# Four chained layers on one core: K/V of the last pairs ahead of their queries at the change of phase

## The reference

```python
x = x + (einsum('bsi,bio->bso', x, W[id]) + b[id])                  # one of 16 experts per sequence
x = x + (x @ W1.T + (x @ A[a].T) @ B[a].T * s[a])                   # W1 shared, adapter a per sequence
x = x + attention(x)                                                # grouped queries, paged cache
x = x + (w3[subject].T mixes the 64 tokens of a sequence) + bias
```

## Time and profile before

| | |
|---|---|
| median of 3 runs | 934.08 us (932.72 to 934.34) |
| profiled execution | 935.61 us, span 933.8 us |
| PE / DVE / ACT / POOL busy | 890.7 / 648.5 / 442.8 / 529.0 us |
| chain that ended last | PE 77%, DVE 7%, DMA 6% |
| mean granted clock | 0.991 |

### The profile page before, as it was taken

The page is one execution under the profiler, slowest core; times in us unless marked ns, Lnnn a source line. Parts: engine busy times, 40 slices in busy tenths (PEclk is TensorE's granted clock), DMA queues, the critical chain, the costliest instruction groups (busy, mean ns, idle before and its releaser), DMA issues.

```text
span 933.8 us, 23545 instructions
## 1 busy us (share of the span) xinstructions
PE 890.7 (95%) x6501; PEld 654.8 (70%) x6501; DVE 648.5 (69%) x1858; ACT 442.8 (47%) x1190; POOL 529.0 (57%) x499
## 2 busy tenths in 40 slices
PE   5599999999999999999996899999999999999997
PEld 3357667666666676676676677878778778777785
DVE  3545445778787764466755778888778887787874
ACT  1424333333333333333423666666666676666762
POOL 2044655655746557865467666655666656666630
PEclk9889999999999999999999999999999999999999
DMA  9999988787887978887716766676766776666741
GB/s 285 300 285 333 332 303 294 258 286 258 264 291 241 295 252 273 307 269 263 250 64 214 209 205 193 194 211 189 214 194 193 210 222 206 198 199 202 227 133 47
DMA packets 100417, 218.55 MB, mean 234 GB/s; under 512 B 30187, under 2 KB 36168, under 8 KB 92178
## 3 DMA queue, kind: packets, MB, share of 16 engines
q1 hardware_dynamic: 66290, 145.27, 47.4%
q0 software_dynamic: 25088, 57.74, 21.5%
q10 hardware_dynamic: 8992, 15.00, 4.4%
HBM read 210.39 MB, written 33.86 MB: 262 GB/s over the span
## 4 chain that ended last, share of the span: by engine, by line
PE 77%; DVE 7%; DMA 6%; SPq 3%; issue 3%; ACTq 2%; ACT 2%; POOL 1%; DVEq 0%; POOLq 0%
PE banks L697 14%; PE banks L847 9%; PE banks L610 9%; PE banks L799 9%; PE banks L835 7%; PE banks L822 6%; PE banks L678 5%; PE banks L776 4%; DMA pair_b<-in_lb 4%; PE banks L883 3%; PE banks L840 3%; DVE later L1166 2%; PE banks L663 2%; PE banks L777 1%; PE banks L815 1%
## 5 line engine op out<-in xcount | busy, mean ns | idle before, releaser
L569 POOL DMA_INDIRECT ring<-new_rows,idx x128 | 129.3, 1010 | 81.1 <-PE banks L799 45.8
L1050 ACT ACTIVATE big<-big,neg_max 128x320 f32<-128x320 f32 x256 | 141.5, 555 | 4.7 <-DVE neg_max L1417 4.4
L1417 DVE CUSTOM_DVE_ANT_0 big<-banks,mask 128x320 f32<-128x320 f32 x256 | 114.6, 486 | 23.6 <-PE banks L799 22.5
L610 PE MATMUL banks<-ring 128*64 128x512 f32 x512 | 119.5, 609 | 11.5 <-DMA ring<-in_w 11.5
L497 POOL TENSOR_TENSOR rms<-ss,neg_half 128x12 f32<-128x12 f32 x30 | 68.5, 2283 | 70.3 <-DVE ss L1356 70.3
L1040 ACT ACTIVATE kt<-banks 128x384 f32<-128x384 f32 x128 | 61.8, 483 | 92.9 <-PE banks L777 92.8
L495 POOL TENSOR_TENSOR ring<-ring 128x512 f32<-128x512 f32 x30 | 38.7, 1291 | 87.4 <-DVE ring L1237 87.4
L558 POOL DMA_INDIRECT ring<-new_rows,idx x64 | 61.5, 961 | 47.0 <-PE banks L822 42.7
L799 PE MATMUL banks<-kt,q_in 64*128 64x128 f32 (+2 forms) x768 | 86.7, 358 | 1.3 <-ACT kt L1040 1.3
L1454 DVE TENSOR_SCALAR big<-big,recip 128x320 f32<-128x320 f32 x256 | 85.7, 397 | 2.3
L610 PEld LDWEIGHTS banks<-ring 128*64 128x64 f32 x512 | 35.0, 140 | 68.8 <-issue 67.5
(11 more groups left out here) (172 smaller groups left out, 2011.3 us busy)
## 6 DMA issues: line engine op xcount, KB each, us to landing
ring<-in_w SPq DMA_DIRECT2D x62, 1024.0 KB, 8.0
ring<-in_xt SPq DMA_DIRECT2D x32, 256.0 KB, 2.7
x_in<-in_x SPq DMA_DIRECT2D x32, 256.0 KB, 5.8
bias_in<-in_b SPq DMA_DIRECT2D x64, 128.0 KB, 8.0
x_dram<-x SPq DMA_DIRECT2D x32, 256.0 KB, 8.8
q_dram<-q_t ACTq DMA_DIRECT2D x32, 256.0 KB, 6.5
new_rows<-kv_out SPq DMA_DIRECT2D x32, 256.0 KB, 6.4
q_in<-q_dram SPq DMA_DIRECT2D x32, 256.0 KB, 2.8
```

The lines of the kernel that those rows point to most:

```text
L569: pool.indirect_dma_start(out=kv[:, s, c, :], out_offset=None, in_=new_rows, in_offset=bass.IndirectOffsetOnAxis(ap=idx[:, b, 1 + c:2 + c] ...
L610: last = nc.tensor.matmul(ps_l0[T * h:T * h + T, :], xt[:, s, c, T * h:T * h + T], w0[:, 2 * s + h, c * D:(c + 1) * D], start=(c == 0), st ...
L1050: nc.scalar.activation(prob[:, s % 2, PLACE[g] * NK:(PLACE[g] + 1) * NK], sm[:, s % 2, g, :], ACT.Exp, bias=neg_max[:, s % 2, g:g + 1], sc ...
L1417: V.tensor_tensor_reduce(sm[:, s % 2, g, :], ps_s[g], mask[:, s % 2, k0:k0 + NK], 1.0, 3.0e38, ALU.add, ALU.min, accum_out=neg_max[:, s % ...
```

## The change

The end of phase one is written anew. LATE = 29 names the first of the last three pairs. K/V of pairs 29 to 31 are computed and stored first; the query products of these pairs stand behind them, and their rotations and transposes follow; those of pairs 30 and 31 stand partly inside the batches 0 to 2. To make that possible, several things change places: the query products of 30 and 31 go to other banks; the turned x2 of pair 30 gets a buffer of its own (`held_hi`, `held_lo`), for which the second row buffer now shares memory with `same`; the row preparation (make_rows, shift_rows, transposes, indices) goes one step earlier; the own half of the mask is loaded once into `own_mask` and written by ScalarE; the 74 dummies become 14; the splits of Wo go into batches 1 and 2; `bd` is cleared later.

```diff
-ROW_STEP = NP - 5
+ROW_STEP = NP - 6
+LATE = NP - 3
-WARM, WARM_X, WARM_T, WARM_Q, WARM_KEYS = 9, 6, 6, 24, 26
+WARM, WARM_X, WARM_T, WARM_KEYS = 9, 6, 6, 14
-        rows = [sb(f"rows{i}", [P, ROWLEN]) for i in range(2)]
+        rows = [sb("rows0", [P, ROWLEN]), same[:, :, :].rearrange("p m r -> p (m r)")[:, 0:ROWLEN]]
...
 (SyncE)
+            sp.dma_start(own_mask, a["own"]).then_inc(ld_mask, 16)
...
-            for s in range(2):
-                sp.dma_start(mask[:, s, 0:T], a["own"]).then_inc(ld_mask, 16)
-                sp.dma_start(mask[:, s, NK:], a["own"]).then_inc(ld_mask, 16)
...
 (GpSimd; steps of phase one no longer finish pairs 29 and up)
+            last_pow(NP - 3, 1)
             make_table(NP - 1, 1, NP // 2)
-            last_pow(NP - 2, 8, 12, 1)
             pool.wait_ge(idx_ready, 1)
+            pool.wait_ge(l0_done, NP - 1)
+            for b in range(KV_EARLY - 2):
+                gather_old(b)
+            last_pow(NP - 2, 1)
             pool.wait_ge(l0_done, NP)
-            for b in range(KV_EARLY - 1):
+            for b in range(KV_EARLY - 2, KV_EARLY):
                 gather_old(b)
-            last_pow(NP - 1, 8, 12, 3)
-            gather_old(KV_EARLY - 1)
-            last_pow(NP - 2, 0, 8, 2)
-            pool.wait_ge(h_done, NP)
-            pool.wait_ge(kv_done, NP)
-            pool.wait_ge(q_done, NP)
-            nc.gpsimd.memset(bd[:, :, :], 0.0).then_inc(pool_set, 1)
-            last_pow(NP - 1, 0, 8, 4)
+            last_pow(NP - 1, 1)
+            pool.wait_ge(st_kv[0], NP // 2 * 16)
+            last_pow(NP - 3, 0)
...
-            for s in range(2):
-                pool.wait_ge(st_kv[s], NP // 2 * 16)
+            pool.wait_ge(st_kv[1], NP // 2 * 16)
             gather_new(0)
+            pool.wait_ge(q_done, NP)
+            nc.gpsimd.memset(bd[:, :, :], 0.0).then_inc(pool_set, 1)
             for b in range(1, NB):
                 gather_new(b)
+                if b <= 2:
+                    last_pow(NP - 3 + b, 0)
...
 (TensorE, behind step 30)
+            adapt_down(NP - 2, 0)
+            experts(NP - 1, NP // 2 - 1, 1)
+            adapt_up(NP - 2, 0)
+            project_kv(NP - 3)
+            transpose_x1(NP - 1, 1)
+            transpose_x2(NP - 2, 0)
+            transpose_queries(NP - 4, 0)
+            project_q(NP - 3, (0,))
             adapt_down(NP - 1, 1)
-            project_kv(NP - 2)
+            project_hidden(NP - 1)
+
             adapt_up(NP - 1, 1)
-            project_q(NP - 2, (0, 1))
+            project_kv(NP - 2, (0, 1))
             transpose_x2(NP - 1, 1)
-            project_q(NP - 2, (2,))
+            project_kv(NP - 2, (2,))
             project_kv(NP - 1)
+            project_q(NP - 3, (1, 2))
+            project_q(NP - 2)
+            project_q(NP - 1)
             transpose_queries(NP - 3, 1)
-            project_q(NP - 1)
             pe.wait_ge(x1_ready, NP)
-            keep_warm(WARM_Q)
-            transpose_queries(NP - 2, 0)
-            keep_warm(WARM_Q)
-            transpose_queries(NP - 1, 1)
+            keep_warm(WARM_KEYS)
...
 (TensorE, end of a batch's step)
+                if isinstance(b, int) and 1 <= b <= 2:
+                    transpose_queries(LATE + b, (LATE + b) % 2)
+                if isinstance(b, int) and b == 2:
+                    pe.wait_ge(qt_ready, NP)
...
 (ScalarE; the queries of 30 and 31 are copied and stored at the end of its steps 1 and 2)
+            for k0 in (0, NK):
+                last = nc.scalar.activation(mask[:, :, k0:k0 + T], own_mask.unsqueeze(1).to_broadcast([P, 2, T]), ACT.Copy)
+            last.then_inc(mask_set, 1)
...
 (VectorE)
-            SIDE = {2: take_tables, ROW_STEP: make_rows, NP - 1: take_indices}
+            SIDE = {2: take_tables, ROW_STEP: make_rows, NP - 2: take_indices}
...
+            def turn(k, w):
+
+                last_squares(k, w)
+                rotate_parts(k, k % 2, w)
+                last_sum(k, w)
...
+            split_x2(NP - 1)
+            turn(NP - 2, 1)
+            last_product(NP - 2, 1)
+            turn(NP - 1, 1)
+            last_product(NP - 1, 1)
+            turn(NP - 3, 0)
+            last_squares(NP - 2, 0)
+            last_product(NP - 3, 0)
             rotate_parts(NP - 2, 0, 0)
...
             last_sum(NP - 2, 0)
...
 (VectorE, end of a batch's step)
+                if isinstance(b, int) and b <= 1:
+                    last_product(LATE + 1 + b, 0)
+                if isinstance(b, int) and b == 0:
+                    turn(NP - 1, 0)
+                if isinstance(b, int) and 1 <= b <= 2:
+                    for c in range(2):
+                        split_wo(2 * b - 2 + c)
```

More of the change, by code:

```diff
@@ L159, in build @@
             x1t_hi, x1t_lo, x2t_hi, x2t_lo = (sb(n, [P, DC, P], F32R, first) for n in ("x1t_hi", "x1t_lo", "x2t_hi", "x2t_lo"))
+            held_hi, held_lo = (sb(n, [P, DC, P], F32R, first) for n in ("held_hi", "held_lo"))
         q_in = sb("q_in", [P, 4, GP, P])
@@ L255, in is_last, with late, q_bank, kv_bank @@
             return isinstance(pair, int) and pair == NP - 1
+        def late(k, first=LATE):
+            return isinstance(k, int) and k >= first
+        def q_bank(k):
+            return (ps_kv, ps_l1)[k - LATE - 1] if late(k, LATE + 1) else ps_q
+        def kv_bank(k):
+            return ps_t1 if late(k, NP - 1) else ps_kv
+        def turned_bank(k):
+            return (ps_la, ps_l1, ps_l1)[k - LATE] if late(k) else ps_t3
+        def x2t_parts(k):
+            if late(k, NP - 1):
+                return x1t_hi, x1t_lo
+            return (held_hi, held_lo) if late(k, NP - 2) else (x2t_hi, x2t_lo)
         def on(n, lag, count):
@@ L403, in phase_two @@
             def phase_two(b, j, s):
+                if isinstance(b, int) and b == 4:
+                    for t in range(2):
+                        sp.wait_ge(st_q[t], (NP // 2 - t) * 16)
+                if isinstance(b, int) and b == 2:
+                    sp.wait_ge(pool_set, 3)
                 if s % 2 == 0 and on(b, -2, NB):
@@ L476, in make_table @@
                 pool.wait_ge(ld_cs[s], CS_DMAS * 16 * loads)
[L477 to L478 removed]
+                if not late(k, NP - 1):
+                    wait(pool, abq_ready, k - 1)
+                    wait(pool, abk_ready, k - 1)
                 if isinstance(k, int) and k == 0:
                     pool.wait_ge(gains_ready, 1)
[L481 removed]
+                out = last_tab if late(k, NP - 1) else tab[:, s, :, :, :]
+                nc.gpsimd.tensor_tensor(out.rearrange("p w f n -> p w (f n)"),
                                         gains[:, :, :, :].rearrange("p w f n -> p w (f n)"),
@@ L641, in transpose_queries @@
                 wait(pe, qt_ready, k)
+                if late(k, LATE + 1):
+                    pe.wait_ge(abq_ready, NP)
+                    pe.wait_ge(sqq_ready, NP)
+                elif late(k):
+                    pe.wait_ge(xa_ready, NP)
+                out = turned_bank(k)
                 for c in range(DC):
-                    last = nc.tensor.transpose(ps_t3[:, c * P:(c + 1) * P], q_rot[:, s, c * P:(c + 1) * P], ident[:, :])
+                    last = nc.tensor.transpose(out[:, c * P:(c + 1) * P], q_rot[:, s, c * P:(c + 1) * P], ident[:, :])
                 last.then_inc(t3_done, 1)
@@ L687, in project @@
             def project(k, ps_out, n0, parts):
-                x_hi, x_lo = (x1t_hi, x1t_lo) if isinstance(k, int) and k == NP - 1 else (x2t_hi, x2t_lo)
+                x_hi, x_lo = x2t_parts(k)
                 if 0 in parts:
@@ L701, in project_q @@
             def project_q(k, parts=(0, 1, 2)):
-                if 0 in parts:
+                if late(k, NP - 1):
+                    pe.wait_ge(x2_ready, NP)
+                elif late(k, NP - 2):
+                    pe.wait_ge(abk_ready, NP - 1)
+                    pe.wait_ge(sqv_ready, NP - 1)
+                elif 0 in parts:
                     wait(pe, abq_ready, k)
@@ L708, in project_q, with project_kv @@
                         pe.wait_ge(wqkv_lo_ready, 1)
-                last = project(k, ps_q, 0, parts)
+                last = project(k, q_bank(k), 0, parts)
                 if 2 in parts:
                     last.then_inc(q_done, 1)
-            def project_kv(k):
-                wait(pe, abk_ready, k)
-                wait(pe, sqv_ready, k)
+            def project_kv(k, parts=(0, 1, 2)):
+                if late(k, NP - 1):
+                    pe.wait_ge(x1lo_ready, NP)
+                elif 0 in parts:
+                    wait(pe, abk_ready, k)
+                    wait(pe, sqv_ready, k)
                 if isinstance(k, int) and k == 0:
@@ L719, in project_kv @@
                     pe.wait_ge(wqkv_lo_ready, 2)
-                project(k, ps_kv, D, (0, 1, 2)).then_inc(kv_done, 1)
+                last = project(k, kv_bank(k), D, parts)
+                if 2 in parts:
+                    last.then_inc(kv_done, 1)
             def phase_one(k, j, s):
```

199 lines of the change are left out of this document (110 added, 89 removed).

## The result

The changed kernel takes 940.72 us (median of 7 runs, 939.55 to 945.21); the kernel before, measured beside it, 933.91 (median of 7, 931.42 to 936.61). The ratio is 1.0071, 95% interval 1.0049 to 1.0092: slower, by 6.8 us. The forecast was 941.9 in 935.0 to 946.5. The profiled execution took 940.93 us.

The account below looks back on a forecast made before the run. TensorE is full on both sides, so any delay ahead of the full batches delays the end. Terms -7.1 + 5.5 - 1.0 + 2.0 + 6.9 + 1.5 = +7.8 gave 941.9 us, range 935.0 to 946.5.

Parts of the forecast that it names:

- the two places: Places left open near the change: the change of phase (13.9 us gap) and the start of the batches (TensorE works 21.34 of 27.5).
- part 1: End of phase one: pair 31's K/V ready earlier, so the gather starts and the keys come earlier, -7.1 us.
- Part 2: Step 26: row preparation one step earlier makes VectorE wait for table_i and TensorE for x1t_lo, +5.5 us.
- the -1.0 of the next step: Step after the stall: shift_rows finds its adapter rows already there, so TensorE's earlier 0.99 us loss goes, -1.0 us.
- Part 3: Phase one behind the stall: TensorE's granted clock drops after the pause, +2.0 us (1.7 to 2.8).
- Parts 4 and 5: First batches: query work in VectorE's queue delays them, +6.9 us; the pause before the keys costs clock, +1.5 us.
- VectorE's 1.9 and 1.25: Work behind batch 1's mask (a product, two wo_lo quarters), 1.9 us, and behind batch 2's, 1.25, counted as delay.
- the clock would cost one batch 1.5 us: First batch: after a 4.8 us rest before the keys, transposes and scores run up to twice as long, +1.5 us.
- 60 fewer dummies cost nothing: Change of phase: fewer dummies cost and give nothing, as all stand before the same wait for the gather.
- Rival 2: First batches: the clock stays low until the full batches, 3 us more than the sum, 945 us; chance 0.13.
- 6.65 was written: VectorE's work added behind the masks of batches 0 to 2: 3.5, 1.9 and 1.25 us, in all 6.65.

Follow-up runs that it names:

- experiment 1: Changed kernel with the writer-table store and the eleven gathers of table_i one GpSimd step earlier: 935.51 us, ratio 1.0010 to the kernel before.
- experiment 2: Kernel before with only the row preparation one step earlier (ROW_STEP at 26): 938.49 us, ratio 1.0051 to the kernel before.
- experiment 6: Changed kernel with 38 dummies on TensorE before the wait for x1t_lo in step 26: 941.73 us (4 runs), ratio 1.0083 to the kernel before.
- kernel 5: Changed kernel with pair 30's product and pair 31's turn ahead of the first masks, GpSimd's powers for both one batch earlier: 940.24 us, ratio 1.0062.
- experiment 4: Changed kernel with the Wo splits moved from batches 1 and 2 to behind the first mask: 940.86 us, ratio 1.0060 to the kernel before.
- experiment 3: Changed kernel with 36 dummies before the keys instead of 14: 938.94 us, ratio 1.0046 to the kernel before.
- 7: Changed kernel with table gathers a step earlier, 38 dummies before the keys, Wo splits and queries of pairs 30 and 31 ahead: 931.24 us, ratio 0.9981.
- 8: Changed kernel with table gathers a step earlier, 38 dummies before the keys and Wo splits ahead, queries left inside the batches: 933.71 us, ratio 0.9991.
- 9: Changed kernel with table gathers a step earlier, 38 dummies and queries of pairs 30 and 31 ahead, Wo splits left in the batches: 934.23 us, ratio 0.9998.
- kernel 10: Changed kernel with table gathers a step earlier, Wo splits and queries of pairs 30 and 31 ahead, 14 dummies kept: 931.69 us, ratio 0.9972.

## Why the prediction was right, and where it was not

The direction, the two places and the waits in them were as written. That the number came within 1.2 us is in part luck. By the trace the change is worth 5.3 us with the start's -1.8 in it, 7.1 without, where 7.8 was written. The terms behind it were off in both directions: part 1 gave 1.6 us more than forecast and the stall with its clock cost 1.0 less, while the first batches cost 0.6 more and the full batches 1.3, which the sum did not have at all.

**Part 1, the order at the end (-7.1 forecast, -8.7 measured).** The end of pair 31's K/V came 4.9 us earlier, 4.75 forecast (its 2.85 us for twelve matmuls is from start to start; to the end of the last they are 3.01). The gather started 7.1 us earlier once the shift of 3.7 us at that point is taken off (496.21 against 499.60), as forecast, though by two errors that cancel: the store was issued 0.6 us later than written (492.6) and landed in 3.3 us instead of 4.0. The rest is the gather's flight to the keys, 5.83 us instead of 7.41. GpSimd, as forecast, was through with the query power in time, and waited for the store's landing:

```profile
493.53 1.64 POOL L568 TENSOR_TENSOR rms<-ss,neg_half 128x8 f32<-128x8 f32 x1 [1.67 <-DVE ss L1336]
496.21 1.03 POOL L593 DMA_INDIRECT ring<-new_rows,idx  x1 [1.05 <-DMA new_rows<-kv_out]
```

One wait was not foreseen. ScalarE's copy of pair 31's values (timeline of ScalarE after) waits for pair 29's store to leave the same buffer, which had been issued at 483.9:

```profile
490.43 0.39 ACT L1021 ACTIVATE kv_out<-banks 128x256 f32<-128x256 f32 x1 [1.26 <-DMA new_rows<-kv_out]
```

That store took 6.5 us to land, where pair 29's took 2.0 before. From its issue to the place of pair 31's copy it was 5.3 us, 6.2 before, so most of this wait is the slow landing and the smaller part the denser order. I had walked only the store of pair 31.

**Part 2, the stall (+5.5 forecast).** The idle was 4.69 us; place, chain and releaser were as written. With the clock behind it and the -1.0 of the next step, 6.5 in the forecast, it is worth 5.2 by experiment 1, 4.5 by experiment 2. The gathers landed at 406.3 instead of 408.9, but VectorE and TensorE were 1.8 us earlier in this execution, so the stall came out only 0.8 short. The -1.0 was met in size, not in its place: step 27 took 0.4 us more than before, and then the waits for x1t_lo of 0.99, 0.31 and 0.27 us in steps 28 to 30 shrank to a single one of 0.27.

**Part 3, its clock (+2.0).** 1.5 by the groups in experiment 6, or 1.8 by the trace of after (6.5 less 4.69 of idle). It is not the same in every execution: in kernel 5 the same stall, 4.74 us of idle, was followed by 7.92 us from the third part to adapt_up, against 6.70 after and 5.05 before, so there it cost 2.9. (Experiment 1 gets both back and loses the -1.0 again: 6.5 less 1.0 is 5.5, and 5.2 was measured.)

**Parts 4 and 5, the first batches (+8.4 forecast, +9.0 measured).** The sum was right, the account of it in part. Batch 1 came 3.5 us late, and 3.53 of query work stood on VectorE in front of its mask, as forecast. For batches 2 and 3 I had added VectorE's 1.9 and 1.25. They did come 2.2 and 1.6 late, but experiment 4 shows that at batch 2 taking the 1.28 away changes nothing: beside VectorE's queue ran a second chain as long, TensorE at half clock. In kernel 1, where the clock was back at 1.00 by 518, VectorE's queue alone sets the mask of batch 2, without idle and 7.89 us behind batch 1's, 1.8 more than before:

```profile
518.21 1.28 DVE L1488 TENSOR_TENSOR wo_lo<-stage,wo_hi 128x512 fp32r<-128x512 f32 x2
519.41 0.48 DVE L1517 CUSTOM_DVE_ANT_0 big<-banks,mask 128x320 f32<-128x320 f32 x1
```

So VectorE's 1.9 was the right size, and the second chain added 0.4 us on top of it after. At batch 3 the split had most of its price by itself (1.0 of 1.28 in experiment 4).

The step that failed is the sentence that the clock would cost one batch 1.5 us. It fell to 0.50 for 502 to 508 (keys to mask 5.68 us instead of 3.82, +1.9, near the forecast), and a second time to 0.56 for 520 to 526, around the end of 4.12 us of idle. That idle came from the query work: TensorE waited for ScalarE's copy (`pt`), which stood behind the first exponential of batch 1, and that one waited for VectorE's late mask. The sentence of part 1 that 60 fewer dummies cost nothing holds for the wait only: 22 more of them took 1.1 us off the time from keys to mask (experiment 3). Rival 2, which I gave 0.13, described the second fall in part; but as the two chains lie side by side, they came out nearly as one delay, not as the sum that it would have given (945). Experiments 7 to 9 price what was moved by the first to the fifth mask: 2.3 us for the queries and 2.5 for Wo, 4.7 together, where 6.65 was written; the product of pair 31 stayed inside in all of them.

The Trainium skill ("TensorE: Matmul & The Clock Gate", section What's actually happening) says "the default state is throttled, and activity releases the throttle". The traces here agree in part: with 0.42 us of idle before the keys (experiment 3) the thin first batches still fell to 0.50, but those of the kernel before, as thin, kept 1.00.

**Open.** The drift of 1.3 us over the full batches. It is not chance: from the first to the thirtieth of TensorE's last-layer products it is 373.2 us before and in experiment 2, and 374.5 to 374.6 after and in kernels 1, 4 and 5 to 10. So it comes with the change, not with ROW_STEP, and no other edit here removes it; its cause is not shown. What is left in the first batches: even kernel 10 needs 28.0 us from the first mask to the fifth, against 23.9 before; its batch 1 comes 8.9 us behind batch 0, with half clock and with keys that waited 2.0 us, by GpSimd's order for gathers standing behind a power. Putting these gathers in front was not tried.

## What to carry to other kernels

When a step is moved earlier, check the due time of what it reads on every queue: here the side work of GpSimd stayed where it was, and one constant cost 5 us, most of the loss. Work that is moved out of a gap into a ramp has the price of its engine's queue there, but one edit alone may show little of it while a second chain is as long; take both away before calling work free. And a gain at the change of phase (8.7 us of earlier keys) is worth keeping only if what was displaced finds room: with the table on time and the queries and splits ahead of the masks, the same change (kernel 10) is faster than before by 0.28% (0.15 to 0.41).

## What the runs showed of the hardware

- TensorE's granted clock fell behind pauses of 0.42, 0.58 and 0.67 us between thin pieces of 1 to 12 matmuls (kernel 3: 0.50 from 502 to 508, TensorE busy 4.75 of 6 us), and did not fall behind one of 2.23 us in the kernel before (idle to 497.99, clock 1.00), nor in the same thin batches there. With 36 or 38 dummies ahead the fall began 2.8, 4.9, 2.0 and 7.7 us behind the start of the keys (kernels 3, 7, 8 and 9), so dummies put it off by an amount that varies and did not remove it.
- The same gathers of the table, issued by the same code: from the last issue to VectorE's cast it was 6.7 us after (399.63 to 406.31) and 8.0 in kernel 6 (400.54 to 408.56), so a stall behind a small indirect transfer is worth a range, not a number.
- The clock behind one and the same stall (4.7 us of idle) cost 1.65 us in one execution and 2.9 in another (after, kernel 5).
